# A linear-attention and expert layer: V and G ahead of the scores, other banks for the scores, a projection in column halves

## What is computed

```
q, k, v, g = x @ Wq, x @ Wk, x @ Wv, x @ Wg
gk = log_sigmoid(x @ Wgk + bgk) / 16
A = einsum(q * dk**-0.5, k) * where(mask, exp(gc_t - gc_s), 0)  # gc = cumsum(gk) in a chunk
o = A @ v                                                       # inside a chunk
for each chunk:  o += (q * exp(gc)) @ S;  S = exp(gt) * S + (k * exp(gt - gc)).T @ v
on = o * rsqrt(mean(o * o) + eps) * gnorm_w
x + (on * silu(g)) @ Wo + experts(x)
```

## Time and profile before

| | us |
|---|---|
| median of 3 runs | 391.74 (391.71 to 392.69) |
| the profiled execution | 392.97 |
| its span in the trace | 391.2 |
| TensorE busy in the span | 373.5 (95%) |
| VectorE | 312.9 (80%) |
| ScalarE | 291.9 (75%) |
| GpSimd | 278.1 (71%) |

### The profile page before, as it was taken

How to read it: one execution, slowest core, us unless ns; L and a number is a source line. 1 busy time by engine, 2 the same in 40 slices (tenths; PEclk the granted TensorE clock), 3 DMA queues, 4 the chain that set the end, 5 groups by cost and what they waited for, 6 DMA issues and landing times.

```text
span 391.2 us, 13871 instructions
## 1 busy us (share of the span) xinstructions
PE 373.5 (95%) x3947; PEld 321.4 (82%) x3947; DVE 312.9 (80%) x859; ACT 291.9 (75%) x889; POOL 278.1 (71%) x245
## 2 busy tenths in 40 slices
PE   7997899999999999999999999999999999999991
PEld 7666677778787878787878777899999999999991
DVE  5987799988888888888888879677777687787761
ACT  4887886888888888888878886566666666666670
POOL 8002353788778888888788883178888888888887
PEclk9996999999999999999999999999999999999997
DMA  8935579555655535575655333146555555555540
GB/s 232 253 137 160 183 226 335 152 172 182 169 179 177 164 107 159 171 189 164 191 164 170 105 103 85 41 67 75 67 72 69 64 72 72 70 75 70 71 41 6
DMA packets 59107, 51.45 MB, mean 132 GB/s; under 512 B 7201, under 2 KB 51393, under 8 KB 59073
## 3 DMA queue, kind: packets, MB, share of 16 engines
q1 hardware_dynamic: 45936, 42.07, 37.5%
q0 software_dynamic: 12272, 8.54, 15.8%
q10 hardware_dynamic: 864, 0.40, 0.4%
HBM read 33.14 MB, written 18.30 MB: 131 GB/s over the span
## 4 chain that ended last, share of the span: by engine, by line
PE 85%; DVE 4%; DMA 3%; ACT 3%; issue 2%; SPq 2%; POOL 1%; DVEq 0%; ACTq 0%; POOLq 0%
PE psVG L965 16%; PE psA L977 16%; PE psVG L771 12%; PE psT L859 8%; PE psO L825 7%; PE psQK L757 5%; PE psT L851 4%; PE psVG L790 4%; PE psO L839 4%; PE psKS L814 3%; ACT E L1148 2%; SPq L355 2%; DMA x_all<-in_L_attn_x_dram 1%; POOL out_dram L619 1%; DMA gcB<-decay_rows 1%
## 5 line engine op out<-in xcount | busy, mean ns | idle before, releaser
L619 POOL DMA_INDIRECT out_dram<-yw,sidx x71 | 112.6, 1586 | 28.8 <-DVE yw L1687 11.2
L1148 ACT ACTIVATE E<-gcB,ngc 128x128 f32<-128x128 f32 x256 | 78.4, 394 | 0.4 <-DMA gcB<-decay_rows 0.4
L577 POOL DMA_INDIRECT sorted_rows<-x_all,pos_i x64 | 65.3, 1020 | 13.4 <-issue 13.1
L561 POOL TENSOR_TENSOR rms<-msn,neg_half 128x8 f32<-128x8 f32 x32 | 53.5, 1673 | 24.7 <-DVE msn L1475 16.5
L554 POOL TENSOR_SCALAR_AFFINE_SELECT E<-E 128x1024 f32<-128x1024 f32 x32 | 35.1, 1096 | 42.8 <-ACT E L1148 30.4
L1130 ACT ACTIVATE th<-psVG,x_all 128x256 f32<-128x256 f32 x64 | 26.8, 470 | 21.6 <-issue 11.9
L825 PE MATMUL psO<-v_sb,pr 128*64 128x64 f32 x1024 | 36.3, 225 | 2.7 <-DVE pr L1504 2.7
L977 PE MATMUL psA<-xT_all,v_sb 128*128 x288 | 38.1, 275 | 0.4 <-DVE yb L1685 0.4
L965 PE MATMUL psVG<-xgT,gcB 128*128 128x128 f32 x288 | 38.0, 275 | 0.0
L825 PEld LDWEIGHTS psO<-v_sb,pr 128*64 128x64 f32 x1024 | 34.8, 141 | 3.4 <-issue 3.2
L977 PE MATMUL psA<-xT_all,th 128*128 x280 | 37.5, 277 | 0.1
(11 more groups left out here) (209 smaller groups left out, 943.1 us busy)
## 6 DMA issues: line engine op xcount, KB each, us to landing
gcB<-decay_rows SPq DMA_DIRECT2D x32, 512.0 KB
sorted_rows<-blank SPq DMA_DIRECT2D x12, 396.0 KB, 5.7
xg<-sorted_rows SPq DMA_DIRECT2D x71, 66.0 KB
x_all<-in_L_attn_x_dram SPq DMA_DIRECT2D x16, 256.0 KB, 5.3
out_dram<-res SPq DMA_DIRECT2D x32, 128.0 KB
eqB<-decay_exp_rows SPq DMA_DIRECT2D x32, 64.0 KB
w1b<-in_L_ffn_w_dram SPq DMA_DIRECT2D x8, 256.0 KB
xT_all<-in_L_ffn_w_dram SPq DMA_DIRECT2D x32, 64.0 KB
```

The costliest lines, as they stand in the source:

```text
L561: nc.gpsimd.tensor_tensor(rms[:], msn[:], neg_half[:, 0:2 * H], ALU.pow).then_inc(rms_ready, 1)
L577: nc.gpsimd.indirect_dma_start(out=sorted_dram, out_offset=bass.IndirectOffsetOnAxis(ap=pos_i[:, t:t + 1], axis=0), in_=x_all[:, t, :], in ...
L619: nc.gpsimd.indirect_dma_start(out=out_rows, out_offset=bass.IndirectOffsetOnAxis(ap=sidx[j][:], axis=0), in_=yw[j][:], in_offset=None, bo ...
L1148: last = nc.scalar.activation(E[j][:, k, h * P:(h + 1) * P], gcB[j][:, k * H + h, :], ACT.Exp, bias=ngcf[:, bass.ds((s * 2 + k) * H + h, 1)])
```

## The change

Four things change, all in the attention steps. (1) TensorE makes V and G of the next sequence right behind Q and K, ahead of the scores. (2) The scores of heads 2 and 3 go to the second halves of two banks that also hold first keys and state (`psKS`) and outputs (`psO`), now one tensor `psKO`; the scores so wait for `og`, the copied state and `kd` of VectorE, and the state for the first `pr`. The outputs are summed pair of heads by pair, the first pair behind the first `pr`. (3) The output projection runs as sixteen passes into halves of 64 partitions. (4) `qk_sb` has two buffers. VectorE's order becomes gated, scale_q, decay_k, probs, copy_state, normed, and ScalarE's copy of Q and K comes ahead of the exponentials, which are split in two halves, one behind V.

```diff
-        qk_sb = sb("qk_sb", [P, 2 * SEQ])
-        kT = qk_sb[:, SEQ:2 * SEQ]
+        qk_sb = [sb(f"qk_sb{j}", [P, 2 * SEQ]) for j in range(2)]
+        kT = [t[:, SEQ:2 * SEQ] for t in qk_sb]
...
-        psKS = ps("psKS", [P, 512])
+        psKO = ps("psKO", [P, 2, 512])
+        psKS, psO = psKO[:, 0, :], psKO[:, 1, :]
         psA = ps("psA", [P, 2, 512])
-        psO = ps("psO", [P, 512])
...
-        ps_pair = [psA, psVG]
+        ps_scores = [psA[:, :, 0:SEQ], psKO[:, :, SEQ:2 * SEQ]]
...
                     pe.wait_ge(gate_ready, s)
-                    if not (isinstance(i, int) and s - 1 in BY_HALVES):
-                        pe.wait_ge(p_ready, (s - 1) * 2 + 1)
...
             def scores(i, j):
                 s = i * 2 + j
                 pe.wait_ge(p_ready, s * 2)
-                pe.wait_ge(gate_ready, s + 1)
+                pe.wait_ge(og_ready, s)
+                pe.wait_ge(s_copied, s)
+                pe.wait_ge(kd_ready, s + 1)
...
-                        last = nc.tensor.matmul(ps_pair[h // 2][:, h % 2, k * P:(k + 1) * P], kT[rows_h, k * P:(k + 1) * P], qk_sb[rows_h, k * P:(k + 1) * P],
+                        last = nc.tensor.matmul(ps_scores[h // 2][:, h % 2, k * P:(k + 1) * P], kT[j][rows_h, k * P:(k + 1) * P], qk_sb[j][rows_h, k * P:(k + 1) * P],
...
+                if not (isinstance(i, int) and s in BY_HALVES):
+                    pe.wait_ge(p_ready, s * 2 + 1)
...
+            def own_pair(i, j, r, first):
+                for k in range(2):
+                    for h in (2 * r, 2 * r + 1):
+                        for c in range(2):
+                            t = k * SEQ + h % 2 * P + c * P // 2
+                            nc.tensor.matmul(psO[c * P // 2:(c + 1) * P // 2, k * HV + h * DV:k * HV + (h + 1) * DV], pr[:, r, t:t + P // 2],
+                                             v_sb[j][:, k, h * DV:(h + 1) * DV], start=(first and k == 0 and h == 2 * r), stop=False,
+                                             skip_group_check=True)
...
-                own_half(i, j, 0)
-                own_half(i, j, 1)
+                first, second = (0, 1) if isinstance(i, int) and s in BY_HALVES else (1, 0)
+                pe.wait_ge(p_ready, s * 2 + 1)
+                own_pair(i, j, first, True)
+                pe.wait_ge(p_ready, s * 2 + 2)
+                own_pair(i, j, second, False)
...
-                        last = nc.tensor.matmul(psT[:, k * D:(k + 1) * D], oT[:, 2 * k + a, :], wo_sb[:, a, :],
-                                                start=(a == 0), stop=(a == 1))
+                        for c in range(2):
+                            last = nc.tensor.matmul(psT[c * P // 2:(c + 1) * P // 2, k * D:(k + 1) * D], oT[:, 2 * k + a, c * P // 2:(c + 1) * P // 2],
+                                                    wo_sb[:, a, :], start=(a == 0), stop=(a == 1), skip_group_check=True)
...
             def step(i, j, extra=None, ahead_of_outputs=None):
                 first_keys(i, j)
                 proj_qk(*turn(i, j, 1, 2))
+                proj_vg(*turn(i, j, 1, 2))
                 scores(i, j)
                 project_out(*turn(i, j, -2, 2))
                 if extra:
                     extra()
-                proj_vg(*turn(i, j, 1, 2))
                 state(i, j)
...
-                if not (isinstance(i, int) and s == 0):
-                    act.wait_ge(k0_ready, s)
+                if isinstance(i, int) and s == 1:
                     act.wait_ge(a_ready, s * 2)
+                if not (isinstance(i, int) and s < 2):
+                    act.wait_ge(k0_ready, s - 1)
+                    act.wait_ge(a_ready, (s - 1) * 2)
...
-                    exp_dec(*turn(i, j, 1, 2))
                     copy_qk(*turn(i, j, 1, 2))
+                    exp_half(*turn(i, j, 1, 2), 0)
                 if aside:
                     aside()
                 if inside(i, j, 1, SEQS):
                     tanh(*turn(i, j, 1, 2))
                     copy_v(*turn(i, j, 1, 2))
+                    exp_half(*turn(i, j, 1, 2), 1)
...
-                if inside(i, j, 0, SEQS):
-                    probs(i, j)
-                    decay_k(i, j)
-                if behind_keys:
-                    behind_keys()
                 if inside(i, j, -1, SEQS):
                     gated(*turn(i, j, -1, 2))
                 if inside(i, j, 1, SEQS):
                     scale_q(*turn(i, j, 1, 2))
+                if inside(i, j, 0, SEQS):
+                    decay_k(i, j)
+                    probs(i, j)
+                if behind_keys:
+                    behind_keys()
+                if inside(i, j, 0, SEQS):
+                    copy_state(i, j)
                 if inside(i, j, -1, SEQS):
                     normed(*turn(i, j, -1, 2))
-                if inside(i, j, 0, SEQS):
-                    copy_state(i, j)
```

46 lines of the change are left out of this document (20 added, 26 removed).

## The result

The changed kernel took **432.54 us** (median of four runs, 430.72 to 433.36), against 392.22 for the kernel before beside it (391.71 to 397.26). The ratio is 1.1036, with a 95% interval of 1.1008 to 1.1064. The forecast was 401.0 us with a range of 391.5 to 405.5: the direction was right, the size was wrong by a factor of four. The profiled execution has a span of 430.1 us.

The account below looks back on a forecast made before the run. TensorE bounds the kernel at 6.50 us a step; VectorE's round of 6.75 takes over: 22 x 0.25 = 5.5 us, plus 3.8 in early steps, together +9.3 on the median 391.74, so 401.0 us, range 391.5 to 405.5.

Parts of the forecast that it names:

- TensorE as the bound before, 6.50 us a step: Attention steps before the change: TensorE's groups follow without a hole and set the step at 6.50 us.
- The column halves, 0.95 us (bounds 0.91 to 1.08): Output projection on TensorE: sixteen half passes take 0.95 us, near enough to the time before the change.
- VectorE's round, 6.75 us: Attention steps: VectorE waits for scores, its round becomes the bound at 6.45 + 0.30 = 6.75 us, +0.25 a step.
- The mask on x_lo, 0.30: VectorE's x_lo overlaps GpSimd's mask by 0.44 us in every round, which costs 0.30 us.
- Steps 2 to 7, +3.8 us: Early steps with VectorE's routing work and little slack: the new hole and the collision add 3.8 us.
- The other engines ... I cost these at nothing: ScalarE, GpSimd and SyncE in the attention stage: their work stays covered and adds 0 us.
- The column halves don't run side by side: Rival, output projection: sixteen passes cost twice 0.91 us, 25 us on top, 426 us; chance 0.03.
- The mask misses x_lo: Rival, VectorE's round: x_lo keeps its 0.42 us, +0.9 us in all, 392.6 us; chance 0.15.
- TensorE stays the bound: Rival, attention steps: scores needn't wait for VectorE, the step is TensorE's 6.36 us, 387.8 us in all; chance 0.08.
- More than forecast: Rival, mask on x_lo: whole 0.44 overlap lost, 404.9 us, or more if GpSimd falls behind; chance 0.07.
- What would show it: Signs in the trace: gates 6.7 to 6.8 us apart, 0.9 idle before first `pr`, x_lo 0.7, early stretch 4 longer.
- The sign given for a wrong forecast: Output projection on TensorE: its sixteen passes taking more than 1.1 us would show the forecast wrong.

Follow-up runs that it names:

- the last experiment: Changed kernel without placements, GpSimd's mask in steps 6 to 28 also waiting until VectorE's x_lo is done: 404.9 us, against 402.0 without this wait.

## Why the prediction was wrong, step by step

**TensorE as the bound before, 6.50 us a step.** I took its groups, which "follow each other without a hole", as TensorE's own work. Without placements the same work takes 6.30 us. The other 0.21 were stalls, and they can't be seen in the earlier trace rows, because a stalled matmul counts as busy until a modelled end. That 19.97 of 20 us were busy was no proof. So the 9.3 us that were forecast for the change compare with 402.0 - 385.5 = 16.5, when neither kernel has placements.

**The column halves, 0.95 us (bounds 0.91 to 1.08).** Right where no placement runs beside them: in the kernel before they changed nothing in a step, and from the first matmul to the update, latency included, they take 1.12 us in the changed kernel. Beside one placement it is mostly 1.8, beside two mostly 3.1. The bounds came from four half passes in the earlier trace rows that ran undisturbed, and nothing in them reached to this.

**VectorE's round, 6.75 us.** The links hold to some hundredths. In the changed kernel without placements they are: gate to x_lo 0.60 (forecast 0.61), x_lo to msn 1.44 (1.22 and 0.30 for the collision), msn to og 0.08 (0.09), og to qe 0.60 (0.59), qe to kd 0.20 (0.20), kd to the first `pr` 1.18 (0.28 + 0.15 + 0.76 = 1.19), from there to S 1.27 (1.21 + 0.07), S to on 0.34 (0.34), on to res 0.60 (0.60), res to the next gate 0.33 (0.33). The sum is 6.64, the measured step 6.65. Of the 0.11 too much, 0.08 are in x_lo to msn: x_lo took 0.72 as forecast, but the 1.22 already held a short wait of the reduction behind it, which started 0.40 after x_lo there and starts 0.34 after an x_lo of the same length in the last experiment. The mechanism, that the wait for the scores closes VectorE's round on itself, is what happens: 0.90 of idle time before the first `pr`, released by the scores, and TensorE waiting 0.27 for `kd`.

**The mask on x_lo, 0.30.** Right in size (0.72 in place of 0.42), but not a price that goes away when the overlap does, as the last experiment shows. The Trainium skill, page "SBUF — State Buffer", section "Who interferes with whom", has a VectorE instruction with two SBUF inputs block for as long as a GpSimd instruction that reads SBUF holds the shared port. The runs agree but for a constant: x_lo and msn lose their overlap with the mask's row less 0.13 to 0.15 us, each time (x_lo 0.24 of 0.37 before and 0.30 of 0.44 in the changed kernel without placements, msn 0.37 of 0.52 in the last experiment).

**Steps 2 to 7, +3.8 us.** Without placements in the changed kernel, steps 2 to 8 take 97.71 - 50.99 = 46.7 us, 5.4 more than the 41.35 of before: somewhat under-sized; against the 40.52 of before without placements it is 6.2 more. With placements it is 50.8.

**"The other engines ... I cost these at nothing".** This is the step that failed. GpSimd's instructions were followed for what they hold on GpSimd and on VectorE's port (the mask), but the placements were not looked at: where they stood in time before, and what of TensorE they would stand beside after. Before, a step's first placement ran under V and G, which no run shows to suffer. The trace of before has only 16 of the 32 updates of V and G, but ScalarE's tanh, which waits for them, starts 0.16 us after their modelled end for every sequence from 5 to 30, as in the run without placements. Here is one that starts while the placement still runs (V and G end at 125.44):

```profile
124.82 1.03 POOL L577 DMA_INDIRECT sorted_rows<-x_all,pos_i  x1 [0.20 <-issue]
...
125.60 0.84 ACT L1130 ACTIVATE th<-psVG,x_all 128x256 f32<-128x256 f32 x2 [0.54 <-PE psVG L771]
```

The change takes V and G away from there and puts the projection, the state and the own passes in their place. The earlier trace rows holds the V and G passes from 130.28 to 131.93; the trace of before has placements at 130.97 and 132.32, and in the changed kernel they stand beside the projection and the state. The lateness in sum went from 8.7 us (scores 3.0, outputs 5.7) to 34.8 on the projection, which the state behind it inherits, and that is the missing 30 us: 401.0 forecast, 402.0 measured without placements, 432.5 with them. That 401.0 and 402.0 nearly meet is partly luck, since a round forecast 0.10 us too long makes up for the early steps.

**The rivals.** "The column halves don't run side by side" gave 426 us, the time nearest to the measured one, and is wrong as a cause: with halves in the kernel before nothing is lost, and without placements the changed kernel's halves are on time. It came from the Trainium skill, page "TensorE: Matmul & The Clock Gate", section "Part 3: Packing small matmuls — row/col tiling", that weight loads overlap only where row groups differ. By that sentence alone, sixteen half passes would take twice as long; the table of measured speedups in the same section, which the prediction left out, has three column tiles 2.38 times as fast. The run with halves alone agrees with the table: it has a step of 6.50 us against 6.51. "The mask misses x_lo" and "TensorE stays the bound" didn't occur. "More than forecast", with GpSimd falling behind, was right in naming GpSimd and wrong in the way.

**What would show it.** Met: the 0.9 us of idle time, the wait for kd, x_lo at 0.72, the expert stage. Not met: gates 6.7 to 6.8 us apart (8.6 and 7.2 by turns; 6.63 to 6.74 without placements), and the early stretch some 4 us longer (9.5; 5.4 without placements). The sign given for a wrong forecast, a projection of more than 1.1 us, is what came, though only its semaphore shows it: its rows still say 0.92 from the first matmul to the state.

**What stays open.** Why an indirect DMA on GpSimd stalls TensorE, and why V, G, Q and K, whose operands are fp32r and whose passes are 512 and 256 columns wide, don't suffer while the f32 passes do. (Q and K were late by 0.6 us once, in the run with four placements in a row, and by 0.1 us once in the kernel before and in each of three versions of it; about half of their updates are missing in these traces.) It is not the bytes moved, not the row's length alone, not the bound on row numbers. What sets the scatters apart, beside which no stall begins, wasn't found. Nor is it shown directly whether the passes themselves stand still or only the report of their end; the holes of 0.46 and 0.43 us in the own passes, which wait for nobody there, speak for the first. No version here beats the kernel before beyond what can be measured: with the same work its best is 391.1 us.

## What to carry to other kernels

When TensorE looks busy without a hole, compare when its semaphores are updated with where its rows end; a releaser named "remote" behind a matmul that the rows call done was this stall here. When a change moves passes of TensorE, lay GpSimd's indirect DMAs over the new order too: what stood under them before may have been the one thing that didn't suffer. And a collision that is moved away can land on the next instruction: the mask, taken off x_lo, met msn and cost 0.37 us in place of 0.30.

## What the runs showed of the hardware that was not expected

- Indirect DMAs that GpSimd issues, of about 1.0 us each, held up TensorE: 64 of them cost 30.5 us in the changed kernel and 5.7 in the one before. A plain DMA of the same rows from GpSimd, 0.58 us each, cost nothing that can be seen. The Trainium skill, page "SBUF — State Buffer", section "Who interferes with whom", gives TensorE ports of its own that it shares with no engine and names the pair of VectorE and GpSimd as the only contention; the runs show TensorE held up by GpSimd, by whatever way.
- TensorE's rows run on through such a stall: in the step shown above, the 16 passes of the projection, 4 of the state and 21 of the own passes have rows that start before 132.0 us, though the projection's update came at 133.47. The holes called "issue" come only behind these.
- V and G passes of 512 columns ran on time under the placements that met them, by their updates and, where these are missing, by tanh behind them, at most 0.16 us after their modelled end in the versions of the kernel before.
